# Attention over 4096 pixels on one core: score products moved to the head of TensorE's steps, VectorE's small operations written in the three-operand form, statistics and g products in other steps

## What is computed

```python
x0 = x
x = _gn(x)                                        # 32 groups of 8 channels
g_x = einsum('oc,bcn->bno', g_w, x) + g_b         # 128 channels
f = einsum('bnc,bcm->bnm', x^T, x)                # 4096 x 4096, symmetric
y = einsum('bnm,bmc->bnc', softmax(f, -1), g_x)
wy = einsum('oc,bcn->bon', W_w, y^T) + W_b
wy = (wy - mean) * rsqrt(var + 1e-5) * gamma + beta   # over images and pixels
return x0 + (wy + x)
```

## Time and profile before

| | us |
|---|---|
| median of 3 runs | 2146.11 (2144.88 to 2146.47) |
| the profiled execution | 2147.57 |
| its span, first to last instruction | 2145.8 |
| TensorE busy | 2043.7 (95%) |
| VectorE busy | 1573.0 (73%) |
| ScalarE busy | 1088.6 (51%) |
| GpSimd busy | 811.2 (38%) |
| mean granted TensorE clock | 0.992 of full speed |

### The profile page before, as it was taken

How to read it: one execution, slowest core, us unless ns; L and a number is a source line. 1 busy time by engine, 2 the same in 40 slices (tenths; PEclk the granted TensorE clock), 3 DMA queues, 4 the chain that set the end, 5 groups by cost and what they waited for, 6 DMA issues and landing times.

```text
span 2145.8 us, 32285 instructions
## 1 busy us (share of the span) xinstructions
PE 2043.7 (95%) x9348; PEld 1455.5 (68%) x9348; DVE 1573.0 (73%) x3123; ACT 1088.6 (51%) x2234; POOL 811.2 (38%) x623
## 2 busy tenths in 40 slices
PE   5999999989999999989999999999999999999887
PEld 4787777656588777656668777766658777766433
DVE  5786777877777777787767777787777777777656
ACT  4344554465435545547454455545543555555544
POOL 4002233558502113448620223345850211345840
PEclk9999999999999999999999999999999999999999
DMA  3222233645421333555522223354642223346969
GB/s 128 113 104 79 94 118 120 200 133 196 153 80 65 113 119 104 181 158 162 186 80 105 79 99 113 123 197 132 196 153 84 75 103 118 117 134 218 342 245 355
DMA packets 108982, 304.48 MB, mean 142 GB/s; under 512 B 11648, under 2 KB 12032, under 8 KB 94976
## 3 DMA queue, kind: packets, MB, share of 16 engines
q1 hardware_dynamic: 108800, 302.30, 40.9%
HBM read 159.65 MB, written 142.61 MB: 141 GB/s over the span
## 4 chain that ended last, share of the span: by engine, by line
PE 66%; issue 18%; POOL 6%; ACT 4%; DMA 3%; DVE 2%; SPq 0%; POOLq 0%; DVEq 0%; ACTq 0%
PE bank L1238 15%; PE bank L1164 9%; PE bank L1166 9%; PE bank L1165 9%; PE bank L1214 7%; PE bank L1242 4%; PE bank L1244 3%; PE bank L1243 3%; PE bank L1388 2%; DMA fy_c<-spill 2%; ACT ring L781 2%; POOL fy_c L714 2%; PE bank L1308 2%; POOL fy_d L714 2%; POOL gl L693 1%
## 5 line engine op out<-in xcount | busy, mean ns | idle before, releaser
L807 ACT CAST phi<-bank 128x512 fp32r<-128x512 f32 x480 | 282.4, 588 | 752.6 <-PE bank L1214 751.1
L958 DVE TENSOR_SCALAR_CACHE_REDUCE ring<-bank 128x512 f32<-128x512 f32 x560 | 385.4, 689 | 285.8 <-PE bank L1166 222.3
L1164 PE MATMUL bank<-xh 128*128 128x512 f32 (+3 forms) x1152 | 512.1, 445 | 7.5 <-POOL xl L687 7.3
L993 DVE TENSOR_TENSOR plo<-bank,phi 128x512 fp32r<-128x512 f32 x480 | 329.4, 686 | 152.5 <-ACT phi L807 108.0
L1166 PE MATMUL bank<-xh,xl 128*128 128x512 f32 (+3 forms) x1152 | 435.7, 378 | 0.0
L1165 PE MATMUL bank<-xl,xh 128*128 128x512 f32 (+3 forms) x1152 | 432.9, 376 | 0.0
L781 ACT ACTIVATE ring<-ring,nmax 128x512 f32<-128x512 f32 x464 | 334.8, 723 | 36.5 <-DVE nmax L985 36.5
L714 POOL TENSOR_TENSOR fy_d<-fy_d,maxrow 128x512 f32<-128x512 f32 x188 | 243.6, 1298 | 263.8 <-DMA fy_d<-spill 263.8
L714 POOL TENSOR_TENSOR fy_c<-fy_c,maxrow 128x512 f32<-128x512 f32 x200 | 261.8, 1311 | 175.8 <-DMA fy_c<-spill 175.8
L1214 PEld LDWEIGHTS bank<-ident,ring 128*128 128x128 f32 x1856 | 223.8, 141 | 146.4 <-issue 84.5
L1214 PE MATMUL bank<-ident,ring 128*128 128x128 f32 x1856 | 282.3, 275 | 14.1 <-DVE plo L993 6.1
(11 more groups left out here) (127 smaller groups left out, 2767.1 us busy)
## 6 DMA issues: line engine op xcount, KB each, us to landing
spill<-ring SPq DMA_DIRECT2D x108, 1024.0 KB, 4.3
fy_c<-spill SPq DMA_DIRECT2D x200, 256.0 KB, 4.0
fy_d<-spill SPq DMA_DIRECT2D x188, 256.0 KB, 3.8
ring<-x_dram SPq DMA_DIRECT2D x40, 512.0 KB, 4.8
lbuf<-spill SPq DMA_DIRECT2D x60, 256.0 KB, 3.7
yd<-yn SPq DMA_DIRECT2D x32, 256.0 KB, 3.0
fx_a<-x_dram SPq DMA_DIRECT2D x16, 512.0 KB, 8.3
out_dram<-fx_a SPq DMA_DIRECT2D x16, 512.0 KB, 4.5
```

The source lines that it names most:

```text
L807: nc.scalar.copy(phi[:, HI_BUF[n], :], whole(p)).then_inc(hi_made, 1)
L958: last = nc.vector.tensor_scalar(slot_tile(u, t), src, 1.0, None, ALU.mult, ALU.max, accum_out=rowm[:, t, c:c + 1])
L993: nc.vector.tensor_tensor(plo[:, n % LOS, :], whole(p), phi[:, HI_BUF[n], :].bitcast(F32), ALU.subtract).then_inc(lo_made, 1)
L1164: nc.tensor.matmul(dst, xh[:, k, rows], xh[:, k, cols], start=(k == 0), stop=False)
```

## The change

Four things, which do not depend on each other:

1. On TensorE the products of a step stand ahead of its `turn`, in every step.
2. Small VectorE operations with all operands in SBUF, and the first addition of each j in `add_left`, are written as `scalar_tensor_tensor` instead of `tensor_tensor` or `tensor_scalar`. In the last stage of `group` the shift for ScalarE comes first.
3. `STATS_STEP` goes from 157 to 162, 166, 167 to 148 to 151, 157, 164, 166, 167.
4. `G_AT` goes from 3, 7, 11, 15, 19, 24 to 3, 7, 11, 14, 17, 20 (chunks 2 to 7).

```diff
-STATS_STEP = [max(X_STEP[c] + 6, X_STEP[-1] + c - 4) for c in range(NB)]
+STATS_STEP = [COLS_STEP[5] + 2 + c if c < 4 else X_STEP[c] + (12 if c == 5 else 6) for c in range(NB)]
...
-G_AT = {T * (c - 1) - (1 if c < NB - 1 else 0): c for c in range(2, NB)}
+G_AT = {min(T * (c - 1) - 1, 3 * c - 1): c for c in range(2, NB)}
...
-                    nc.vector.tensor_tensor(gnp[:, bass.ds(n, 1), 0, :].rearrange("p b k -> p (b k)"), gst[:, 0, :],
-                                            gst[:, 3, :], ALU.mult)
+                    gn_scale = gnp[:, bass.ds(n, 1), 1, :].rearrange("p b k -> p (b k)")
+                    gn_shift = gnp[:, bass.ds(n, 1), 0, :].rearrange("p b k -> p (b k)")
                     nc.vector.scalar_tensor_tensor(out=gst[:, 4, :], in0=gst[:, 0, :], scalar=-1.0, in1=gst[:, 3, :],
                                                    op0=ALU.mult, op1=ALU.mult)
-                    nc.vector.tensor_scalar(gnp[:, bass.ds(n, 1), 1, :].rearrange("p b k -> p (b k)"), gst[:, 3, :],
-                                            1.0, None, ALU.add).then_inc(gnp_made, 1)
+                    nc.vector.scalar_tensor_tensor(out=gn_shift, in0=gst[:, 0, :], scalar=1.0, in1=gst[:, 3, :],
+                                                   op0=ALU.mult, op1=ALU.mult)
+
+                    nc.vector.scalar_tensor_tensor(out=gn_scale, in0=neghalf[:, :], scalar=-2.0, in1=gst[:, 3, :],
+                                                   op0=ALU.mult, op1=ALU.add).then_inc(gnp_made, 1)
...
-                    nc.vector.tensor_tensor(own_max, mx[:, 0, :], mx[:, 1, :], ALU.max).then_inc(max_own, 1)
+                    nc.vector.scalar_tensor_tensor(out=own_max, in0=mx[:, 0, :], scalar=1.0, in1=mx[:, 1, :], op0=ALU.mult, op1=ALU.max).then_inc(max_own, 1)
...
-                nc.vector.tensor_scalar(nmax[:, j % 3, :], own_max, -1.0, None, ALU.mult).then_inc(max_made, 1)
+                nc.vector.scalar_tensor_tensor(out=nmax[:, j % 3, :], in0=own_max, scalar=-2.0, in1=own_max,
+                                               op0=ALU.mult, op1=ALU.add).then_inc(max_made, 1)
...
-                    nc.vector.tensor_tensor(lacc, left_at(w), left_at(of[0]), ALU.add).then_inc(left_added, 2)
+                    nc.vector.scalar_tensor_tensor(out=lacc, in0=left_at(w), scalar=1.0, in1=left_at(of[0]), op0=ALU.mult, op1=ALU.add).then_inc(left_added, 2)
...
-                    nc.vector.tensor_tensor(lsum[:, :], lside[:, :], lsum[:, :], ALU.add).then_inc(summed, 1)
+                    nc.vector.scalar_tensor_tensor(out=lsum[:, :], in0=lside[:, :], scalar=1.0, in1=lsum[:, :], op0=ALU.mult, op1=ALU.add).then_inc(summed, 1)
...
+                for x3 in PRODUCTS_AT[p]:
+                    multiply(b, *x3)
+                if more and p in NEXT_PRODUCTS:
+                    multiply(b + 1, *NEXT_PRODUCTS[p])
                 if p + LAG < TILES:
                     turn(b, p + LAG, first)
                 elif more:
                     turn(b + 1, p + LAG - TILES)
-                for x3 in PRODUCTS_AT[p]:
-                    multiply(b, *x3)
-                if more and p in NEXT_PRODUCTS:
-                    multiply(b + 1, *NEXT_PRODUCTS[p])
                 attend(b, p, first)
```

More of the change, by code:

```diff
@@ L245 @@
 X_STEP = [last_use(LAST_IN_SLOT[X_SLOT + c // 2]) + 1 + c % 2 for c in range(NB)]
-STATS_STEP = [max(X_STEP[c] + 6, X_STEP[-1] + c - 4) for c in range(NB)]
+STATS_STEP = [COLS_STEP[5] + 2 + c if c < 4 else X_STEP[c] + (12 if c == 5 else 6) for c in range(NB)]
+assert all(s > X_STEP[c] + 5 for c, s in enumerate(STATS_STEP)) and STATS_STEP == sorted(STATS_STEP)
 GROUP_AT = STATS_STEP[-1] + 3
@@ L914, in group @@
                     dve.wait_ge(gn_own, n * 3 + 1)
-                    nc.vector.tensor_tensor(gst[:, 1, :], mv[:, :, 0], gst[:, 0, :], ALU.subtract).then_inc(gn_own, 1)
+                    nc.vector.scalar_tensor_tensor(out=gst[:, 1, :], in0=mv[:, :, 0], scalar=1.0, in1=gst[:, 0, :], op0=ALU.mult, op1=ALU.subtract).then_inc(gn_own, 1)
                     dve.wait_ge(gn_own, n * 3 + 2)
-                    nc.vector.tensor_tensor(gst[:, 1, :], gst[:, 1, :], gst[:, 1, :], ALU.mult).then_inc(gn_own, 1)
+                    nc.vector.scalar_tensor_tensor(out=gst[:, 1, :], in0=gst[:, 1, :], scalar=1.0, in1=gst[:, 1, :], op0=ALU.mult, op1=ALU.mult).then_inc(gn_own, 1)
                     dve.wait_ge(gn_own, n * 3 + 3)
-                    nc.vector.tensor_tensor(gst[:, 1, :], gst[:, 1, :], mv[:, :, 1], ALU.add).then_inc(gn_in, 1)
+                    nc.vector.scalar_tensor_tensor(out=gst[:, 1, :], in0=gst[:, 1, :], scalar=1.0, in1=mv[:, :, 1], op0=ALU.mult, op1=ALU.add).then_inc(gn_in, 1)
                 elif stage == 2:
```

## The result

The changed kernel takes 2151.76 us (median of 9 runs, 2150.55 to 2155.73), the kernel before 2146.47 on the same chip (9 runs, 2140.81 to 2148.67): a ratio of 1.0036, 95% interval 1.0027 to 1.0045. One run of all, 8507.1 us of the kernel e2_forms, is left out of its ratio. The profiled executions took 2150.55 and 2147.57 us, with spans of 2148.8 and 2145.8.

A forecast was written before the change was run, and what follows sets the result against it. TensorE is busy 95% of the span, so the prediction counted only its waits as winnable. Terms summed to -25.3 us from the profiled 2147.6, giving 2122.3, less 1.5: 2121 us, whole range 2111 to 2142.

The forecast's parts named there:

- Step 175: At tile 176's split, four small forms at 0.15 us make VectorE 3.5 us earlier; 4.5 gained three times, -13.5 us.
- Rival A: The new form waits for GpSimd like the old; only g gains, 2142 us; chance 0.16.
- L1026 and L1006: At step 129 both get shorter, so TensorE's L1171 wait of 0.7 us goes in four images: -2.9 us.
- Statistics: Waits around steps 157 to 165 go, -10.7 us; chunks at 148 to 151 add waits, +6.3 us.
- The wait of 2.1 at tile 150: Two chunks ahead of tile 150's split make TensorE wait 2.1 us in three images: +6.3 us.
- g products: At tile 28 the 1.76 us wait for gl goes, tile 29's split is late next; 1.0 an image, -4.0 us.
- Products ahead of the turn: In 56 steps an image with both, product-to-product distance hardly changes: 0 us, bounds -2 and +12.
- The upper bound: For the products ahead of the turn: an exponential in ScalarE's way at five tight spots an image, +12 us.
- The signs to look for: Prediction wrong if small forms still take 1.1 us and more, or tiles wait for splits behind steps with products.

The follow-up runs named there:

- e2_forms: The kernel before with only the small VectorE operations written as scalar_tensor_tensor: 2145.06 us, ratio 1.0002.
- e7_onesided: The kernel before with small operations taking operands from PSUM and three operations of `group` taken out of step 175: 2126.48 us, ratio 0.9920.
- e3_stats: The kernel before with only `STATS_STEP` changed: 2146.98 us, ratio 1.0005.
- e9_onesided_stats: The kernel of e8_onesided_g with the changed `STATS_STEP`: 2123.80 us, ratio 0.9906 to the kernel before.
- e4_g: The kernel before with only `G_AT` changed: 2147.57 us, ratio 1.0012.
- e8_onesided_g: The kernel of e7_onesided with the changed `G_AT`: 2123.76 us, ratio 0.9905 to the kernel before.
- e6_order_kept: The kernel of e1_order with the turn first again in 54 of 256 steps: 2144.35 us, ratio 1.0003 to the kernel before.
- e5_old_order: The changed kernel with the turn back ahead of the products: 2148.10 us, ratio 1.0017 to the kernel before.
- e1_order: The kernel before with only TensorE's order changed, products ahead of the turn: 2157.48 us, ratio 1.0063.

## Why the prediction was wrong, step by step

**Step 175, -13.5: the failed step.** "L928, the one three-operand form among them, takes 0.15 ... and I read L928 as a form that does not" wait. e2_forms puts this term and the next at 0: 1.0002. What makes such an operation long is where its operands lie and whether GpSimd is at work beside it: the sums with one operand in PSUM took 0.165 us at most, where they had taken up to 1.31. Rival A named the mechanism and got 0.16; its price of 2142 rested on g's gain, which did not come either. The rest of the step, "TensorE then has from tile 176 ... the product can start at 966.7. Gain 4.6", held once the operations were short or gone from there: e7_onesided gained 5.1 an image at steps 168 to 184.

The rule that the prediction quoted against this term, in the Trainium skill's page "SBUF — State Buffer", section "Who interferes with whom" (a VectorE instruction with two SBUF inputs contends with a GpSimd instruction that reads SBUF), was right, and form indeed doesn't matter: the trace agrees, with 1.22 and 1.23 us for two elements in the new form and 0.17 for four elements with one operand in PSUM. I had read one row against it. In one point the prediction leaned on it too far: L930, which it counts as agreeing, is a tensor_scalar with one SBUF input, and so is nmax (L985). Both were long all the same, 1.25 and 1.20, and a rule on two inputs does not cover them.

**L1026 and L1006, -2.9: failed with it.** With the sum taken from PSUM, e7_onesided gained 1.0 an image there. The size was right, the means was not.

**Statistics, -10.7 + 6.3.** The wait of 2.1 at tile 150 came: 1.9. But TensorE then ran at a granted clock of 0.62 in the three images of e3_stats, and the place cost 3.8, not 2.1: a mis-sized term. (Where the clock stayed at 1.00, in e9_onesided_stats, it cost 2.2.) The earlier trace rows had shown the same behind the wait at tile 176, and I had counted it there and not here. The old place gave 3.8 instead of 3.2, and the last image gained 1.3. By the profile that makes 3 x 0 - 1.3, by the ratio +1.1 (-0.9 to +3.0).

**g products, -4.0: failed.** The wait for gl left, and "what is late next is the split of tile 29", 0.9, came as 0.99. Missed was a second wait, of 0.93, from rmax, which collides with the earlier gl. By idle time that is 0.93 + 0.99 - 1.76, about 0.2, but the part measured +2.7. Steps 16 to 32 of e4_g grew by 0.8 an image, which is that sum; where the 0.6 beyond the idle time goes no run shows. With the maxima one-sided, the same move is 2.7 faster by the medians (e8_onesided_g), but the starts grew by 0.1 an image at steps 16 to 32 and the intervals of the two kernels overlap: that the move gains is not shown, only that it no longer costs the 0.8.

**Products ahead of the turn, 0: failed.** In microseconds it is the second miss, 12.6 alone behind the 16.4 of the small forms. "Since every step turns the same way, the distance from a product to the next one hardly changes" left out that ScalarE and VectorE serve both in one queue each. Seen in the traces is that queue at step 36; that the other spots are of the same kind is inferred from e6_order_kept. The upper bound (+12, something in ScalarE's way at five spots an image) had the size and nearly the mechanism: there are five spots, of 0.5 to 0.9 us. And "no first matmul of a product ever waited" had read the matmuls' row alone: at 688.99 the weight load of the product already waited 0.44 us for a take.

**The sum.** Measured alone, by their medians, the parts make 0.2 + 2.1 + 2.7 + 12.6 = +17.6 us. Measured together they make 0.36%, 7.7 us: the other three make 0.17% together (e5_old_order), about as alone, and the order adds 0.19% to them where alone it costs 0.63%. Against the -25.3 of the prediction, the small forms with L1026 and L1006 are half of the miss of 33. The signs to look for had been named ("the small forms still take 1.1 us", "tiles wait for their splits"), and the changed profile shows both.

## What to carry to other kernels

One short instruction among long ones is no evidence of a cheap form while its start lies where another engine's instruction ends. Ask what the long ones share, here operands in SBUF only beside an instruction of GpSimd, and take that away: the same sum with one operand in PSUM fell from up to 1.31 to 0.165 us. Doing so, and taking three small operations away from the critical place, brought 17.5 us, renaming them nothing. When work is moved, look for the first time-critical instruction behind its new place: moving the statistics gained nothing with two early chunks ahead of one split, and 9.8 us with the early chunks in VectorE's gaps. A reordering on one engine that leaves its own distances alone still moves what the others do in a fixed order, so follow each queue to the next wait for a bank.

## What the hardware showed that I had not expected

- The wait goes both ways. In e1_order a left addition of VectorE with both operands in SBUF takes 1.54 us, and GpSimd's subtraction beside it 1.74 instead of 1.27:

```profile
995.87 1.54 DVE L1006 TENSOR_TENSOR bank<-lbuf,ring 128x512 f32<-128x512 f32 x1
...
996.81 1.74 POOL L714 TENSOR_TENSOR fy_d<-fy_d,maxrow 128x512 f32<-128x512 f32 x1
```

- A tensor_scalar with one operand (nmax, four elements, SBUF to SBUF) waits as well, for up to 1.28 us at 437.87 in the kernel before. Reading from PSUM it took 0.16.
- A wait of the same length at the same tile does not have the same price. Behind waits of 1.91 to 1.94 us the granted clock showed 0.59 to 0.64 over 4.1 us in five images, that is, part of them at 1.2 GHz, and stayed at 1.00 (2.4 GHz) in four; steps 144 to 152 lost 3.8 us in the first case and 2.1 to 2.2 in the second. Price a new wait with both values as bounds.
